# Two 8-head layers with their two sequences half a trip apart, and the causal ban inside the 16-head row maximum

## The reference, cut to what matters

```
# 16 heads of 16: q, k rotated, then
scores = einsum(q, k) / 4 ; scores[key later than query] = -inf ; attn = softmax(scores)
# each of two layers, 8 heads of 64:
h = shift_token(x)                       # the second half of a row comes from the row before
q, k, v = split(h @ wqkv)                # 256 -> 3 * 512
q = l2norm(q) * qs ; k = l2norm(k) * ks ; q, k = rotary_xpos(q, k)
o = local_attention(q, k, v)             # windows of 128: own window and the one before, causal band
x = x + o @ wo
h = layernorm(shift_token(x)) * lg + lb
a, g = split(h @ w1 + b1)                # 256 -> 2 * 682
x = x + (a * gelu(g)) @ w2 + b2
```

## Time and profile before

| what | us |
|---|---|
| median of 3 runs (2721.39 to 2726.86) | 2722.84 |
| profiled execution: device time / span | 2726.97 / 2725.2 |
| PE busy, share of the span | 2377.3, 87% |
| DVE, ACT, POOL busy | 1564.7, 1206.8, 965.5 |
| up to the layers (0 to 1255) / layers | 1255 / 1470 |
| clock granted to PE, mean over the span | 0.916 |

### The profile page before, as it was taken

The page is one execution under the profiler, slowest core; times in us unless marked ns, Lnnn a source line. Parts: engine busy times, 40 slices in busy tenths (PEclk is TensorE's granted clock), DMA queues, the critical chain, the costliest instruction groups (busy, mean ns, idle before and its releaser), DMA issues.

```text
span 2725.2 us, 46487 instructions
## 1 busy us (share of the span) xinstructions
PE 2377.3 (87%) x16770; PEld 1799.0 (66%) x16770; DVE 1564.7 (57%) x4242; ACT 1206.8 (44%) x3055; POOL 965.5 (35%) x1367
## 2 busy tenths in 40 slices
PE   7999699977888888886788898898888988988988
PEld 4666599965464555545567676686676766866766
DVE  5555422225647566546657558567675585585754
ACT  1112133324755555653624636437345354372362
POOL 2222122214443333323715416236155262462442
PEclk9999699987988879788899998998999989989999
DMA  3222311121010100003000000000010000000000
GB/s 123 93 100 97 106 38 36 39 71 32 3 58 7 47 18 33 2 10 111 2 16 16 17 16 1 17 16 33 16 57 16 26 8 32 16 2 32 16 2 32
DMA packets 75794, 96.31 MB, mean 35 GB/s; under 512 B 6141, under 2 KB 68946, under 8 KB 75314
## 3 DMA queue, kind: packets, MB, share of 16 engines
q1 hardware_dynamic: 70642, 81.72, 8.9%
q0 software_dynamic: 3408, 9.31, 1.2%
q10 hardware_dynamic: 1520, 2.31, 0.2%
HBM read 62.51 MB, written 30.28 MB: 34 GB/s over the span
## 4 chain that ended last, share of the span: by engine, by line
PE 30%; DVE 14%; POOL 4%; issue 3%; ACT 2%; DVEq 0%; POOLq 0%; ACTq 0%
PE l_bank L1977 6%; PE l_bank L1978 5%; PE l_bank L1979 5%; PE l_bank L2084 4%; POOL l_probs L1622 3%; DVE l_work L1699 3%; DVE l_ss L1680 2%; PE l_bank L2019 2%; PE l_turned L2037 2%; PE l_bank L2053 2%; DVE l_probs L1697 1%; DVE l_probs L1718 1%; PE l_turned L1977 1%; PE l_turned L1978 1%; PE l_turned L1979 1%
## 5 line engine op out<-in xcount | busy, mean ns | idle before, releaser
L1622 POOL TENSOR_SCALAR l_probs<-l_probs,l_rinv 128x256 f32<-128x256 f32 (+1 forms) x512 | 223.3, 455 | 129.0 <-DVE l_rinv L1723 127.9
L1058 DVE TENSOR_REDUCE c_cnmax<-cbank 128x1 f32<-128x384 f32 (+3 forms) x384 | 206.2, 595 | 108.5 <-PE cbank L1249 89.5
L1896 ACT ACTIVATE l_probs<-l_probs,l_nmax 128x256 f32<-128x256 f32 (+1 forms) x512 | 238.9, 473 | 0.0
L1158 ACT ACTIVATE c_cprobsT<-cbank 128x384 f32<-128x384 f32 (+1 forms) x384 | 180.5, 522 | 97.9 <-PE cbank L1275 97.1
L1718 DVE CUSTOM_DVE_ANT_0 l_probs<-l_bank,mask 128x256 f32<-128x256 f32 (+1 forms) x512 | 169.1, 387 | 37.3 <-PE l_bank L2019 22.8
L1606 POOL TENSOR_TENSOR l_work<-l_work 128x512 f32<-128x512 f32 x64 | 82.7, 1292 | 272.5 <-DVE l_work L1699 271.6
L979 POOL TENSOR_SCALAR_AFFINE_SELECT c_cprobsT<-c_cprobsT 128x256 f32<-128x256 f32 x256 | 99.4, 412 | 165.9 <-ACT c_cprobsT L1158 163.8
L2019 PE MATMUL l_bank<-l_kT,l_flipped 64*128 64x256 f32 (+1 forms) x1024 | 152.6, 420 | 0.0
L1942 ACT ACTIVATE l_v<-l_bank,l_b 128x512 f32<-128x512 f32 (+1 forms) x96 | 66.1, 689 | 193.0 <-PE l_bank L1979 193.0
L718 PE MATMUL h_bank<-m_xsT,m_w1s 128*128 128x128 f32 x1248 | 148.4, 278 | 0.3 <-issue 0.3
L1977 PE MATMUL l_bank<-l_part,l_w_high 128*128 128x512 f32 (+1 forms) x288 | 123.1, 427 | 26.3 <-DVE l_yT L1789 26.3
(11 more groups left out here) (273 smaller groups left out, 6358.5 us busy)
## 6 DMA issues: line engine op xcount, KB each, us to landing
w<-in_W1T SPq DMA_DIRECT2D x8, 1024.0 KB, 8.3
w<-in_W2T SPq DMA_DIRECT2D x8, 1024.0 KB, 11.3
l_came<-y_d SPq DMA_DIRECT2D x16, 512.0 KB, 4.2
ys_d<-m_y SPq DMA_DIRECT2D x39, 128.0 KB, 1.7
xn_d<-a_prods SPq DMA_DIRECT2D x8, 512.0 KB, 3.1
c_came<-x_d SPq DMA_DIRECT2D x8, 512.0 KB, 4.8
y_d<-c_raw SPq DMA_DIRECT2D x8, 512.0 KB, 3.7
y_d<-l_probs SPq DMA_DIRECT2D x8, 512.0 KB, 3.4
```

Of the source, the lines that this page charges most:

```text
L1058: dve.tensor_reduce(nmax[:, c % 2, qt, s, i:i + n], S, AX, ALU.max, negate=True).then_inc(nmax_ready[s], 1)
L1158: act.activation(probsT[s][:, c % 2, i, k0:k0 + w], turned_place(j, s)[:, 0:w], ACT.Exp).then_inc(probs_ready[s], 1)
L1622: pool.tensor_scalar(probs[s][:, held(u), h, 0:n], probs[s][:, held(u), h, 0:n], rinv[s][:, u, h:h + 1], 1.0, ALU.mult, ALU.mult)\
L1896: act.activation(probs[s][:, held(u), h, 0:n], probs[s][:, held(u), h, 0:n], ACT.Exp, bias=nmax[s][:, u, h:h + 1], scale=-1.0, accum_out=r ...
```

## The change

Four things, all in phase_attn1 and phase_layers:

- The 16-head maximum. The two mask products go; a table `later` (three tiles of zero, one of the causal ban) is set up once, and `row_max` becomes one `tensor_tensor_reduce` for each head, which adds the ban, writes the sum into a part of `raw` that is free then, and keeps the maximum. A unit of two heads takes two instructions. The maximum waits for the one before of its sequence.
- The 8-head layers are no longer run over trips of pairs but over sixteen halves n, one for each sequence and layer. While half n is in its attention, half n-1 is in its hidden layer; then half n is in Wo, residual, shift and norm while n-1 is in its down projection; then half n+1 makes its rotations, and the transposes, affine and split of the norm of half n stand between them. There is a first round without hidden layer and a last one without attention.
- For that, banks and buffers are dealt anew: two score banks, two for transposes (and the down projection), one for outputs (and the shift), three free ones which serve the rotations and then the hidden layer. A step of the attention is one window and four heads of one sequence, eight steps a half, buffers of probabilities in two instead of three places, transposition two steps later instead of three, output three instead of four. Hidden groups are copied out of PSUM at once: g by ScalarE, a by DVE; gelu and gating work on SBUF, all after the last group.
- The order: on ScalarE the exponentials of a step stand ahead of the copy of transposed probabilities; the affine of the norm goes from DVE to ScalarE, and there are three function table loads for each half instead of for each trip; on DVE gating and split stand among the last residuals. Weights come with a semaphore each, and POOL splits them at other places.

```diff
@@ phase_attn1, DVE
-                        S = score_place("scores", u, s)[:].rearrange("p (h k) -> p h k", h=n)[:, :, 0:(qt + 1) * P]
-                        dve.tensor_reduce(nmax[:, c % 2, qt, s, i:i + n], S, AX, ALU.max, negate=True).then_inc(nmax_ready[s], 1)
+                        wide = (qt + 1) * P
+                        ban = later[:, (NT - 1 - qt):NT, :].rearrange("p a b -> p (a b)")
+                        if pair * UNITS + u:
+                            dve.wait_ge(nmax_ready[s], pair * UNITS + u)
+                        for h in range(n):
+                            last = dve.tensor_tensor_reduce(raw[:, CHUNKS - NS + s, h * 2 * P:h * 2 * P + wide], score_place("scores", u, s)[:, h * 2 * P:h * 2 * P + wide], ban, -1.0, 3e38,
+                                                            ALU.add, ALU.min, nmax[:, c % 2, qt, s, i + h:i + h + 1])
+                        last.then_inc(nmax_ready[s], 1)
@@ phase_attn1, PE
-                            for half in range(2):
-                                for s in range(NS):
...
-                                    last = pe.matmul(score_place("scores", u, s)[:, at:at + P], g.mask[r, 3 * half, :], g.mask[r, 3 * half + 2, :],
-                                                     start=False, stop=half == 1)
@@ phase_layers
+        FLIP_LAG, OUT_LAG, SPAN = 2, 3, 11
+        HIDDEN_AT = ((0, 1), (2, 3), (4, 5), (6,), (7,), (8,), (9,), (10,), (11,), (), ())
@@ phase_layers, DVE
+                def rotations(n, between):
...
+                    for t in range(NT + 1):
+                        if t < NT:
+                            turn(t, 0)
+                        if t:
+                            invert(t - 1)
+                        if t < NT:
+                            turn(t, 1)
+                            norms(t)
+                        if t == 1:
+                            between()
...
+                for n in range(HALVES + 1):
+                    att, ffn = n < HALVES, n > 0
+                    for p in range(SPAN):
+                        if att:
+                            if 0 <= p - FLIP_LAG < STEPS:
+                                pT_out(n, p - FLIP_LAG)
+                            if 0 < p <= STEPS:
+                                invert_sums(n, p - 1)
+                            if p < STEPS:
+                                row_max(n, p)
+                        if ffn:
+                            for k in HIDDEN_AT[p]:
+                                if k % 2:
+                                    take_out(n - 1, k)
...
+                        if ffn and p == 8:
+                            gated(n - 1, 0)
+                            gated(n - 1, 1)
+                        if ffn and p == 9:
+                            low_units(n - 1, 0)
+                            gated(n - 1, 2)
+                            low_units(n - 1, 1)
+                            gated(n - 1, 3)
+                            low_units(n - 1, 2)
+                            gated(n - 1, 4)
+                        if p == 9 and n + 1 < HALVES:
+                            low_parts(n + 1)
+                    if ffn:
+                        low_units(n - 1, 3)
+                    if att:
+                        residual(n, 0)
...
+                    if att:
+                        measure(n)
+                    if ffn:
+                        add_rows(n - 1, 1)
+                    if att:
+                        norm(n)
...
+                    if n + 1 < HALVES:
+                        rotations(n + 1, lambda: low_rows(n))
@@ phase_layers, ScalarE
+                    for p in range(SPAN):
+                        if att:
+                            if 0 < p <= STEPS:
+                                exps(n, p - 1)
+                            if ffn and p == 8:
+                                act.preload_act_table(ACT.Gelu)
+                            if 0 <= p - FLIP_LAG < STEPS:
+                                pT_out(n, p - FLIP_LAG)
...
+                        if ffn and p == 8:
+                            gelu(n - 1, 0)
+                            gelu(n - 1, 1)
+                            if n + 1 < HALVES:
+                                rows_out(n + 1)
@@ phase_layers, PE
+                def rotations(n, between):
+                    project(n, 0)
+                    between()
+                    project(n, 1)
+                    flip_qk(n, 0)
+                    project(n, 2)
+                    flip_qk(n, 1)
+                    project(n, 3)
...
+                for n in range(HALVES + 1):
+                    att, ffn = n < HALVES, n > 0
+                    for p in range(SPAN):
+                        if att and p < 2:
+                            scores(n, p)
+                        if ffn:
+                            for k in HIDDEN_AT[p]:
+                                hidden(n - 1, k)
+                        if att and p < 2:
+                            flip_qk(n, p + 2)
+                        if p == 9 and n + 1 < HALVES:
+                            flip_rows(n + 1)
+                        if att and p >= 2:
+                            if p - FLIP_LAG < STEPS:
+                                flip(n, p - FLIP_LAG)
+                            if p < STEPS:
+                                scores(n, p)
+                            if 0 <= p - OUT_LAG < STEPS:
+                                output(n, p - OUT_LAG)
+                            if p == SPAN - 2:
+                                attended(n, 0)
+                                attended(n, 1)
+                    if att:
+                        attended(n, 2)
+                        attended(n, 3)
+                    if ffn:
+                        contract(n - 1, 0, 1)
+                    if att:
+                        shift(n)
+                    if ffn:
+                        contract(n - 1, 1, NT)
+                    if n + 1 < HALVES:
+                        rotations(n + 1, lambda: flip_hn(n))
```

1102 lines of the change are left out of this document (585 added, 517 removed).

## The result

| what | before | after |
|---|---|---|
| median of 4 runs (lowest to highest), us | 2724.69 (2721.39 to 2726.86) | 2752.95 (2752.44 to 2753.78) |
| ratio after to before, 95% interval | | 1.0102 [1.0088, 1.0116] |
| span of the profiled execution, us | 2725.2 | 2750.7 |
| start of the layers (first product) / layers to the end, us | 1254.6 / 1470.6 | 1236.5 / 1514.2 |

The change makes the kernel 1.0% slower; I had forecast 1.5% faster. The two halves of the change go opposite ways: the layers begin 18.0 us earlier and take 43.6 us longer.

A forecast was written before the change was run, and what follows sets the result against it. PE was taken to set the pace, yet idle some 18 us a trip. Layers 69 + 15 x 87.9 + 48 + 3 = 1438.5 (-32) and the 16-head maximum (-8) gave 2683 us, range 2655 to 2705 (chance 0.45).

The forecast's parts named there:

- fed part: Attention, from the first row_max to the last hidden group's end: PE kept supplied with work, 28.6 us a half.
- first half: First round, without hidden layer: 62 us for rotations, attention, Wo, residuals and shift, plus 7 for POOL's weight splits, 69.
- Dense work and rotation: From the start of project(0) to the first row_max: 29.4 us, with PE idle for some 6 of it.
- Tail: From the last hidden group's end through contract: 28.3 us, norm beside contract, gelu's table load on the chain.
- Clock: Each period: 1.5 us added for stretches at the lower clock, bounds 0 and 4.
- Layer 2: Half 8: w1 split before the power with 6 us to spare, 3 us added for the rest.
- Last half: Last round, without attention: norm, hidden layer, gelu and gating, contract, clock and store, 48 us.
- 16-head maximum -8: 16-head stage: PE loses about 33 us of masks, DVE gains 32, net -8 us, bounds -25 and +15.
- C: Rival, chance 0.21: one stream's rotation loop has nothing to fill its waits; period 93, layers 1515, kernel 2759 us.
- a period over 90.6: Layers: break-even half period, 2.7 us above the forecast one; the prediction fails outright if a period exceeds it.
- B: Rival, chance 0.29: forecast waits too strict in tail and k loop, masks were PE's bound; period 84, kernel 2615 us.
- D: Rival, chance 0.05: 16-head stage slower on DVE by 15 us eats the gain; period 89, kernel 2722 us.

The follow-up runs named there:

- e9: Changed kernel with the gates' gelu replaced by the identity with the same bias and its table load left out: 2754.24 us, ratio 1.0139 to the kernel before.
- e4: Changed kernel, but ScalarE copies the second sequence's rows out of PSUM at step 8 of the first half: 2741.69 us, ratio 1.0069 to the kernel before.
- e1: Kernel before with only the new 16-head maximum, its masks gone: 2704.43 us against 2720.36, ratio 0.9945.
- e3: Changed kernel with inverse before next turn on DVE, root before square on ScalarE, k's normalisation before adds on POOL: 2672.73 us, ratio 0.9827 to kernel before.
- e13: Changed kernel with inverse and root first on DVE and ScalarE, POOL's order kept, clamp of the sums left out: 2718.06 us, ratio 0.9993 to kernel before.
- e15: Changed kernel with the new rotation order on DVE, ScalarE and POOL, and the clamp of the sums left out: 2671.49 us, ratio 0.9825 to kernel before.
- e10: Changed kernel with ScalarE's copies out of PSUM ahead of the exponentials in each attention step: 2947.61 us, ratio 1.0855 to the kernel before.

## Why the prediction was wrong

The step that failed is PE's fed part in the attention, priced at 28.6 us and measured at 32.0 in each of three halves at full clock (n = 3, 5 and 13); next comes the first half, priced at 69 and measured at 86.2. In its own steps:

- **Dense work and rotation, up to the first row_max: 29.4, measured 29.4.** Right in the sum, but not in its parts. The 5.66 for a tile holds the clamp's collision of before (1.02 instead of 0.24 in that tile), which I had not seen. In the kernel after the clamp is free and q pays about as much, which is luck. The stalls I gave 0.9 and 1.0 are 1.57 ahead of the second tile's turn and 1.17 ahead of the fourth's. With no collision and the better order the stretch is 25.2.
- **The fed part, 28.6 (28.7 by the cut above), measured 32.0.** This is the step that failed. By starts, PE's stretch from 1717.34 to 1748.32 is 7.6 for seven scores (forecast 6.85), 15.6 for ten hidden groups (14.0), 2.8, 0.8 and 4.2 for flips, flip_qk and outputs (2.7, 0.75, 4.3), and ahead of it 1.07 go by until the first four maxima are there, which I had counted as fed already. A single group between steps costs 1.51 to 1.62, not 1.40, and 1.85 where the flip behind it waits: its first product takes 0.34 to the next, as shown above, instead of 0.24. The 1.40 of the earlier trace rows is the second group of a run of twelve products; the first of that run takes 1.48 and a group alone between transposes 1.47 (1641.35 to 1642.82), so the trace of before held the higher price. Two outputs wait 0.35 each for oT, which is nearly all of what the scores ahead of them have too much. Sum 3.4 a half, 51 us for fifteen if all are like these. The step was not chain-bound: the loop over the scalings showed one wait of 0.17, as the cover by hidden groups said.
- **Tail 28.3, measured 28.4.** Right: norm and power lie beside contract, attended(2) waits for residual(0) (1.42 here). But the table load, which I put on its chain, is not on it (e9). PE's waits came out otherwise, 1.40 for the last scalings and 1.27 for oT where I gave 0.9 and 1.0, and the exact sum is in part luck.
- **Clock 1.5 a half: 1.3 at most.** The mean period is 1.9 above the undisturbed one, of which the ninth half alone makes 0.6; not all of the rest is the clock, since the first period is 1.8 longer at full clock.
- **Layer 2, +3: 9.3.** The w1 split had "6 us to spare" before the power; it had, but it stood on DVE's gating.
- **First half 69, measured 86.2.** Rotation 29.6 (26.5), attention 41.3 (37 with the splits), and from the first Wo to project(1) 15.3 (6). Of this last part 2.2 us are due to low_parts(1) and rows_out(1) behind the last oT copy (e4); DVE is idle for 8.9 us ahead of them. The 6 was too small by its own rows: Wo alone is 7.3 in the sum of the dense work. The mean granted clock in this part is 0.85.
- **Last half 48, measured 51.7.**
- **16-head maximum -8: -16 by e1, -18.0 in the traces.** The maximum costs DVE 12 us in all, where I gave 32: an instruction with the ban is as long as a reduction of the same width (0.688 and 0.684 us at 512 columns, 0.554 and 0.551 at 384, means of 128). My price of the new form was right; that of the old was too low. The row "x4" with 2.22 us shows the shape of its first instruction only: singly it is two reductions of 512 columns (starts 0.61 and 0.60 apart) and two of 384 (0.47), not four of 512 at 0.555. And "a 16-head trip within 2 us of 92" has no row behind it: a trip takes 147.1, and took 152.7.

The ledger of the layers: 1438.5 forecast, + 51 (fed part), - 3 (clock), + 6 (ninth half), + 17 (first), + 4 (last) = 1513.5, against 1514.2. These terms are read from the trace of the kernel after; of the fed part and the last half no run takes the excess away.

**Of the rivals**, C had the sign, and nearly the figure (layers 1515, kernel 2759). Its mechanism is real, as e3 and e13 to e15 show: 4.2 us a half hang on the order of the rotation and the collision in it. But it does not explain the distance to my own sum, since my rotation came out; that is the fed part and the first half. So C was right in its number largely by luck: its period was 93, the measured one 91.7, and the first and the last half, which it took over from my sum, made up the rest. Its sign, DVE idle for over 1 us in every tile, was met in two tiles of four, besides the first product's wait that my sum held. That a period over 90.6 means a slower kernel held. B is refuted for this kernel, D as well.

What stays open: why dips of the clock come in some halves and not in others of one run (83 us of the layers at the lower level in e3, 251 in e10, 115 in the kernel after, which differ by an order alone). The share of the collision is known within the bounds above, not better, since no kernel was free of it with the order of the kernel after. No run tries another place for the hidden groups, the part that failed. That the order of gates' split and sums matters was not tried.

## What to carry to other kernels

When an instruction's time differs between places with equal shapes, look at what the engine beside it does at that moment before pricing anything from it: here the same collision stood at the normalised q (0.94 us), at a clamp of 16 columns (up to 1.03), at the gating (5.7) or at POOL's scalings (0.5 to 0.9), depending on the order, and removing it from one place proved nothing until the durations of all neighbours had been looked at. Where DVE and POOL are released by one event, let DVE's shorter instruction be first; in e3 it was, by 0.04 us; POOL bore the wait (1.56 for 1.04), and the half, with the new order, was 4.3 us shorter. A merged row of a timeline shows the shape of its first instruction: look at the single ones before dividing by the count. Price a matmul group by its distance to the next instruction of the mix in which it will stand, and give the first period of a new pipeline a sum of its own.

## What the hardware showed

- A DVE tensor_tensor with both inputs in SBUF (128x512, 0.69 us) and a scalar_tensor_tensor (0.74) wait until the end of a POOL tensor_tensor that began first: 1.63 behind one of 1.26, and 6.42 behind one of 6.25; a tensor_tensor took 2.77 behind a POOL cast of 2.46. In the other direction POOL's 128x512 multiplication takes 1.56 beside such a DVE instruction and 1.04 without.
- A DVE tensor_scalar of 128x16 from SBUF to SBUF, 0.24, waits in the same way (up to 1.27); reductions (1.21), instructions of DVE that read PSUM (0.68), and the maxima with the ban did not.
- A function table load takes 1.28 (47 of them), and an operation that is ready starts 1.29 after it began, with no further time shown for a drain.
